# A transformer layer on eight cores: attention groups reordered, score banks rotated, a weight load and buffers re-placed

## The chip, the cores and the metric

The kernel runs on the 8 cores of one Trainium2 chip, each core with 2 of the 16 sequences and no traffic between cores. The metric is the device time of the slowest core in microseconds (us), lower is better.

## What is computed

One layer with the normalization behind each residual sum, for x of 16 x 2048 x 1024 (float32):

```python
q, k, v = x @ Wq, x @ Wk, x @ Wv                      # 1024 x 1024 each
scores = where(causal, q @ k.T, -inf) / 32            # 2048 x 2048 per sequence
x = layernorm(x + (softmax(scores) @ v) @ Wo)
h = silu(x @ (w_gate / 127).T) * (x @ (w_up / 127).T)  # hidden width 3072, int32 weights
x = layernorm(x + h @ (w_down / 127).T)
```

## The kernel before

P = 128, S = 2048, D = 1024; a sequence has 16 tiles t of 128 queries, in 4 groups g of four (NT = 16, NG = 4, ND = 8). All matmuls are bf16, 128 x 128 weights against up to 512 columns, into the banks of PSUM: banks 0 to 5 are `PF` (float32, `pf`), 6 and 7 are `PB` (bf16, `pbank`).

`emit_seq` (L333) runs twice, for sequence 0 and 1:

- POOL casts x to bf16 in DRAM and loads `wqb` and `wkb` (L340 to L344); SP loads x transposed, `xT`.
- Q and K projection (L356), each weight tile used for four matmuls in a row; then `wvb` is loaded on POOL (L372) into the place of wqb and wkb, so after the last K matmul; V projection (L380), two matmuls per weight tile.
- `wob`, the output projection's weights, is allocated and loaded on POOL right after V's part of the program (L391, L392), and in sequence 0 the three feed-forward weights are cast to bf16 in DRAM behind it (L395 to L397).
- Attention (L402 to L468). `emit_scores_softmax(t)`: g + 1 banks of scores, 8 matmuls each (L411), bank nb always in PSUM bank nb; the last, diagonal bank is scaled and masked by DVE (L416), the others copied by ACT (L421), all into `sc`; DVE takes the maximum (L425), ACT the exponential into `E` (L428), one of four slots j = t % 4. `emit_T(t)`: 4(g + 1) transposes of E on TensorE (L443), eight to a bank of PB, and a DVE copy into `ET` (L447). `emit_AV(g)`: 8 banks (4 and 5 in turn) of 4(g + 1) matmuls (L456), copied by DVE to `aoT` (L460).
- Output projection (L492) by tiles, with the residual sum (L497) and `emit_ln` (L316) on DVE and ACT; y goes to DRAM (SP, L501) and in bf16 (POOL, L503), and after tiles 7 and 15 SP loads half of it transposed, `yT` (L509).
- Gate and up (L543, L553) in 6 groups of weights `wgTb`, `wuTb` (SP transposes, L528, L532), product into `h`; down projection (L591) with `wdT` (SP transposes, L579), second `emit_ln`, output.

The order of attention is written out:

```python
for g in range(NG):
    for j in range(4):
        emit_scores_softmax(4 * g + j)
    for j in range(4):
        emit_T(4 * g + j)
    emit_AV(g)
```

What waits for what: each engine and each DMA queue works off its instructions in program order. `Builder.op` records for every operation what it must wait for by the keys it reads and writes; instructions on TensorE need not wait for one another. SBUF is laid out by `Arena`: `alloc` takes the start of the smallest free block that is large enough, `free` gives the range back and merges it with free neighbours, and the block then carries the pending operations of all that was in it. Whoever writes into a tensor allocated from the block waits for all of these (alias waits), even where the bytes themselves belonged to something else. 210,815 bytes a partition are handed out. Of them 17,056 hold constants and `xs`; then come xT (32,768), wqb and wkb (16,384 each), qT, kT and v (32,768 each), up to 180,896.

The functions that the change touches, and what calls them:

Of the kernel before, what the change touches and what calls it, by code (L numbers as in the profile page):

```python
# [205 lines left out]
class Arena:  # L206
# [9 lines left out]
        self.live = {}  # L216
        self.peak = 0

    def alloc(self, name, shape, dtype):
        nbytes = int(np.prod(shape[1:])) * mybir.dt.size(dtype)  # L220
        nbytes = (nbytes + 31) // 32 * 32
        for ent in sorted(self.free_list, key=lambda e: e[1]):
            if ent[1] >= nbytes:
                off = ent[0]
                deps = set(ent[2])
                ent[0] += nbytes
                ent[1] -= nbytes
                if ent[1] == 0:
                    self.free_list.remove(ent)
                for nm, (o2, n2) in self.live.items():  # L230
                    assert off + nbytes <= o2 or o2 + n2 <= off, \
                        f"arena overlap: {name}@({off},{nbytes}) vs {nm}@({o2},{n2})"
                h = self.nc.alloc_sbuf_tensor_at(name, list(shape), dtype, offset=self.base + off)
                self.live[name] = (off, nbytes)
                self.peak = max(self.peak, max(o + n for o, n in self.live.values()))
                self.b.add_alias_deps(name, deps)
                return h
        raise MemoryError(f"arena: no space for {name} ({nbytes}B/part); "
                          f"free={[(e[0], e[1]) for e in self.free_list]}")
# [17 lines left out]
def build_program():  # L257
# [6 lines left out]
    wo_d = nc.dram_tensor("wo", [D, D], F32, kind="ExternalInput")  # L264
# [24 lines left out]
    b = Builder(nc)  # L289
    ar = Arena(nc, b)  # L290
# [42 lines left out]
    def emit_seq(s):  # L333
# [41 lines left out]
        for t in range(NT):  # L375
# [7 lines left out]
            for half in range(2):  # L383
# [4 lines left out]
        ar.free("xT" + sfx)  # L388

        aoT = ar.alloc("aoT" + sfx, [P, ND, S], BF16)  # L390
        wob = ar.alloc("wob" + sfx, [P, ND, D], BF16)  # L391
        b.dma("pool", lambda e: e.dma_start(out=wob[:], in_=wo_d.ap().rearrange("(ec p) k -> p ec k", p=P)),  # L392
              writes=[("wob" + sfx,)], key="wo")
        if s == 0:
            b.dma("pool", lambda e: e.dma_start(out=wgbf_d.ap(), in_=wg_d.ap()), writes=[("wgbf",)], key="wgc")  # L395
            b.dma("pool", lambda e: e.dma_start(out=wubf_d.ap(), in_=wu_d.ap()), writes=[("wubf",)], key="wuc")
            b.dma("pool", lambda e: e.dma_start(out=wdbf_d.ap(), in_=wd_d.ap()), writes=[("wdbf",)], key="wdc")  # L397
        scb = ar.alloc("sc" + sfx, [P, S], F32)
        Eb = ar.alloc("E" + sfx, [P, 4, S], BF16)
        ET = ar.alloc("ET" + sfx, [P, NT, 512], BF16)  # L400

        def emit_scores_softmax(t):  # L402
            g = t // 4
            wlen = (g + 1) * 512
            j = t % 4
            sl = t % 2
            for nb in range(g + 1):
                ap, kk = pf(nb * 512, 512)
                for ec in range(ND):
                    b.op("pe", lambda e, ap=ap, ec=ec, t=t, nb=nb:  # L410
                         e.matmul(ap, qT[:, ec, t * P:(t + 1) * P], kT[:, ec, nb * 512:(nb + 1) * 512],  # L411
                                  start=(ec == 0), stop=(ec == ND - 1)),
                         reads=[("qT" + sfx, ec, t // 4), ("kT" + sfx, ec, nb)], writes=list(kk))
                if nb == g:
                    b.op("dve", lambda e, ap=ap, nb=nb, j=j:
                         e.scalar_tensor_tensor(scb[:, nb * 512:(nb + 1) * 512], ap, INV_SQRT_DK,  # L416
                                                maskt[:, j, :], ALU.mult, ALU.add),
                         reads=list(kk) + [("maskt", j)], writes=[("sc" + sfx, nb)])
                else:
                    b.op("act", lambda e, ap=ap, nb=nb:  # L420
                         e.activation(scb[:, nb * 512:(nb + 1) * 512], ap, AF.Copy, scale=INV_SQRT_DK),  # L421
                         reads=list(kk), writes=[("sc" + sfx, nb)])
            sckeys = [("sc" + sfx, nb) for nb in range(g + 1)]
            b.op("dve", lambda e, wlen=wlen, sl=sl:
                 e.reduce_max(nmax[:, sl:sl + 1], scb[:, 0:wlen], axis=AX.X, negate=True),  # L425
                 reads=sckeys, writes=[("nmax", sl)])
            b.op("act", lambda e, wlen=wlen, sl=sl, t=t, j=j:
                 e.activation(Eb[:, j, 0:wlen], scb[:, 0:wlen], AF.Exp, bias=nmax[:, sl:sl + 1], scale=1.0,  # L428
                              accum_out=rs_all[:, t:t + 1]),
                 reads=sckeys + [("nmax", sl)], writes=[("E" + sfx, j), ("rs", t)])  # L430

        def emit_T(t):
            g = t // 4
            ncs = 4 * (g + 1)
            j = t % 4
            for c0 in range(0, ncs, 8):
                cb = min(8, ncs - c0)
                half = (c0 // 8) % 2
                for ci in range(cb):
                    cs = c0 + ci  # L440
                    apb, kkb = pbank(half, ci * P, P)
                    b.op("pe", lambda e, apb=apb, cs=cs, j=j:
                         e.transpose(apb, Eb[:, j, cs * P:(cs + 1) * P], identb[:]),  # L443
                         reads=[("E" + sfx, j), ("identb",)], writes=list(kkb))
                apb, kkb = pbank(half, 0, cb * P)
                dst = ET[:, c0:c0 + cb, j * P:(j + 1) * P]
                b.op("dve", lambda e, dst=dst, apb=apb: e.tensor_copy(dst, apb),  # L447
                     reads=list(kkb), writes=[("ET" + sfx, c0 + ci, j) for ci in range(cb)])

        def emit_AV(g):  # L450
            ncs = 4 * (g + 1)
            for vc in range(ND):
                ap, kk = pf((4 + vc % 2) * 512, 512)
                for cs in range(ncs):
# [5 lines left out]
                b.op("dve", lambda e, ap=ap, vc=vc, g=g: e.tensor_copy(aoT[:, vc, g * 512:(g + 1) * 512], ap),  # L460
                     reads=list(kk), writes=[("aoT" + sfx, vc, g)])

        for g in range(NG):
            for j in range(4):
                emit_scores_softmax(4 * g + j)
            for j in range(4):
                emit_T(4 * g + j)
            emit_AV(g)  # L468
        b.op("dve", lambda e: e.reciprocal(ri_all[:], rs_all[:]),
             reads=[("rs", t) for t in range(NT)], writes=[("ri",)])  # L470

# [44 lines left out]
        ar.free("r1" + sfx)  # L516
        ar.free("y" + sfx)

        h_actT = ar.alloc("h" + sfx, [P, NH, S], BF16)
        wgTb = ar.alloc("wgTb" + sfx, [P, 2, ND, 512], BF16)  # L520
        wuTb = ar.alloc("wuTb" + sfx, [P, 2, ND, 512], BF16)
        sg = ar.alloc("sg" + sfx, [P, 2, 512], BF16)

        for hgrp in range(NH // 4):
            slw = hgrp % 2
# [118 lines left out]
```

How the kernel before makes its waits and increments, by code:

```python
            def body(eng):  # L167
                know = {}
                for o in ops_by_eng[eng_key]:
                    for d in sorted(o.deps):
                        p = ops[d]
                        if p.sem_id is None:
                            continue
                        v = eff_val(p, o.i)
                        if know.get(p.sem_id, 0) >= v:
                            continue
                        sem = dma_sems[p.sem_id[1]] if p.sem_id[0] == "d" else eng_sems[p.sem_id[1]]
                        eng.wait_ge(sem, v)
                        n_waits[0] += 1
                        know[p.sem_id] = v
                        for k, v2 in p.know.items():
                            if know.get(k, 0) < v2:
                                know[k] = v2
                    ins = o.fn(eng)
                    if o.sem_id is not None:
                        ins.then_inc(dma_sems[o.sem_id[1]] if o.sem_id[0] == "d" else eng_sems[o.sem_id[1]],
                                     16 if o.sem_id[0] == "d" else 1)
                    for k, v2 in o.know.items():
                        if know.get(k, 0) < v2:
                            know[k] = v2
                if eng_key == "sp":
                    for k in final_wait_keys:
                        if k in dma_counts and know.get(("d", k), 0) < dma_counts[k]:
                            eng.wait_ge(dma_sems[k], dma_counts[k])
```

## Time and profile before

| | us |
|---|---|
| median of 2 runs | 3381.49 (3380.61 to 3382.38) |
| the profiled execution | 3385.87 |
| its span on the slowest core (core 7) | 3384.3 |
| spans of the 8 cores | 3363.1 to 3384.3 |
| busy on core 7: TensorE, DVE, ACT | 2636.4, 510.9, 320.9 |
| mean granted TensorE clock | 0.746 |

The profile is that of core 7, unless a row says otherwise, with times from the start of its span. PE is TensorE (PEld its weight loads), DVE VectorE, ACT ScalarE, POOL GpSimd, SP SyncE; SPq is SP's queue. L411 is line 411 of the kernel. In a view of instructions, a line gives start, duration, engine, line, operation, output <- inputs and how many are merged into it; the bracket behind gives the engine's idle time just before and who ended it. In a view of windows, a line gives the stretch, its length, then busy time and number of instructions for PE, PEld, DVE, ACT and POOL, the clock granted to TensorE (1.00 is 2.4 GHz, 0.50 is 1.2 GHz), the DMA engines' busy share and GB/s. The trace misses a few matmul records, so "x5" behind "x3" may stand where there are more.

### The profile page before, as it was taken

How to read it: one execution, taken by the hardware profiler on the slowest of the kernel's cores; microseconds unless marked ns; L12 is line 12 of the kernel's file. 1: busy time of each engine (PE TensorE's matmuls, PEld its weight loads, DVE VectorE, ACT ScalarE, POOL GpSimd, SP SyncE). 2: the span in 40 equal slices, each digit the busy share in tenths (PEclk: the TensorE clock that was granted, in tenths of full speed). 3: DMA queues.
4: the chain of work that ended last, by engine and by line, in shares of the span. 5: the costliest groups of instructions: out<-in, count | busy, mean ns of one | idle time of the engine just before them, and what ended most of it. 6: DMA issues, size and time to landing. Idle time of an engine off the chain costs nothing.

```text
span 3384.3 us, 34352 instructions; the slowest of 8 cores (3363.1 to 3384.3 us)
## 1 busy us (share of the span) xinstructions
PE 2636.4 (78%) x8256; PEld 808.4 (24%) x8256; DVE 510.9 (15%) x754; ACT 320.9 (9%) x629; POOL 32.0 (1%) x60
## 2 busy tenths in 40 slices
PE   0779777878870999977966787778788739999599
PEld 0323111111110333322322331111111113333144
DVE  0000211110330111111220001110103211111033
ACT  0212000010000111100001220000100001111000
POOL 0000000000000000000000000000000000000000
PEclk9988555555555999988988995555555559999799
DMA  9129900000457211123243110000004551110423
GB/s 121 35 38 118 112 6 0 0 0 0 118 124 121 45 35 26 26 42 90 88 99 63 21 30 0 0 0 0 0 0 109 118 110 31 26 37 15 81 89 104
DMA packets 254654, 176.31 MB, mean 52 GB/s; under 512 B 224976, under 2 KB 224976, under 8 KB 253648
## 3 DMA queue, kind: packets, MB, share of 16 engines
q1 hardware_dynamic: 240640, 121.68, 15.3%
q0 software_dynamic: 13840, 52.43, 11.6%
q8 instruction: 94, 1.54, 0.2%
q14 instruction: 80, 0.66, 0.1%
HBM read 121.63 MB, written 69.21 MB: 56 GB/s over the span
## 4 chain that ended last, share of the span: by engine, by line
PE 75%; issue 8%; SPq 7%; DMA 6%; DVE 2%; ACT 1%; POOL 0%; DVEq 0%; ACTq 0%; POOLq 0%
PE PF L543 12%; PE PF L553 12%; PE PF L456 11%; PE PF L591 11%; PE PF L411 11%; PE PF L356 7%; PE PF L492 6%; PE PF L380 4%; SPq L347 3%; PE PB L443 2%; SPq L509 2%; SPq L579 2%; DMA xs<-x 2%; DMA xbf<-x 1%; DMA wgTb_s<-wgbf 1%
## 5 line engine op out<-in xcount | busy, mean ns | idle before, releaser
L543 PE MATMUL PF<-yT_s,wgTb_s 128*128 128x512 bf16 x1536 | 413.6, 380 | 140.0 <-DMA wgTb_s<-wgbf 140.0
L456 PE MATMUL PF<-ET_s,v_s 128*128 128x512 bf16 x640 | 365.0, 588 | 89.2 <-DVE ET_s L447 3.2
L591 PE MATMUL PF<-wdT_s,h_s 128*128 128x512 bf16 x1536 | 370.6, 381 | 81.8 <-DMA wdT_s<-wdbf 81.8
L411 PE MATMUL PF<-kT_s,qT_s 128*128 128x512 bf16 x640 | 359.3, 582 | 89.3 <-DVE sc_s L416 5.7
L553 PE MATMUL PF<-yT_s,wuTb_s 128*128 128x512 bf16 x1536 | 410.3, 376 | 0.0
L492 PE MATMUL PF<-wob_s,aoT_s 128*128 128x512 bf16 x512 | 290.0, 590 | 78.5 <-DVE r_s L497 11.6
L356 PE MATMUL PF<-xT_s,wqb_s 128*128 128x512 bf16 x512 | 123.9, 388 | 165.1 <-DMA xT_s<-xbf 156.6
L565 DVE TENSOR_TENSOR h_s<-PF,sg_s 128x512 bf16<-128x512 f32 x192 | 123.7, 686 | 788.9 <-PE PF L553 781.5
L543 PEld LDWEIGHTS PF<-yT_s,wgTb_s 128*128 128x128 bf16 x1536 | 146.7, 96 | 392.7 <-issue 303.8
L591 PEld LDWEIGHTS PF<-wdT_s,h_s 128*128 128x128 bf16 x1536 | 149.1, 97 | 303.1 <-issue 168.8
L553 PEld LDWEIGHTS PF<-yT_s,wuTb_s 128*128 128x128 bf16 x1536 | 146.7, 96 | 249.2 <-issue 159.2
L416 DVE SCALAR_TENSOR_TENSOR sc_s<-PF,maskt 128x512 f32<-128x512 f32 x32 | 22.1, 692 | 972.7 <-PE PF L411 877.6
L562 ACT ACTIVATE sg_s<-PF 128x512 bf16<-128x512 f32 x192 | 104.2, 594 | 670.1 <-PE PF L543 670.0
L380 PE MATMUL PF<-wvb_s,xT_s 128*128 128x512 bf16 x512 | 134.9, 384 | 37.0 <-DMA wvb_s<-wv 37.0
L456 PEld LDWEIGHTS PF<-ET_s,v_s 128*128 128x128 bf16 x640 | 66.6, 105 | 384.5 <-issue 383.4
L411 PEld LDWEIGHTS PF<-kT_s,qT_s 128*128 128x128 bf16 x640 | 66.1, 105 | 381.0 <-issue 379.4
L356 PE MATMUL PF<-xT_s,wkb_s 128*128 128x512 bf16 x512 | 120.8, 379 | 8.2 <-ACT kT_s L361 2.4
L492 PEld LDWEIGHTS PF<-wob_s,aoT_s 128*128 128x128 bf16 x512 | 51.3, 105 | 316.8 <-issue 316.3
L443 PE MATMUL PB<-identb,E_s 128*128 128x128 bf16 x320 | 81.4, 266 | 50.4 <-DVE ET_s L447 9.8
L356 PEld LDWEIGHTS PF<-xT_s,wqb_s 128*128 128x128 bf16 x512 | 50.7, 99 | 237.6 <-issue 189.2
L460 DVE CAST aoT_s<-PF 128x512 bf16<-128x512 f32 x64 | 44.3, 692 | 410.5 <-PE PF L456 410.5
L325 ACT ACTIVATE lnl<-mv,epsb 128x1 f32<-128x1 f32 x64 | 18.8, 294 | 915.7 <-DVE mv L321 915.7
(42 smaller groups left out, 687.1 us busy)
## 6 DMA issues: line engine op xcount, KB each, us to landing
xs<-x SPq DMA_DIRECT2D x32, 512.0 KB, 5.2
ydram<-y_s SPq DMA_DIRECT2D x32, 512.0 KB, 3.0
ys_s<-ydram SPq DMA_DIRECT2D x32, 512.0 KB, 4.1
out<-outb_s SPq DMA_DIRECT2D x32, 512.0 KB, 2.9
xbf<-x POOLq DMA_DIRECT2D x2, 4096.0 KB, 41.2
ybf<-y_s POOLq DMA_DIRECT2D x32, 256.0 KB, 6.3
wgbf<-wg POOLq DMA_DIRECT2D x1, 6144.0 KB, 86.8
wubf<-wu POOLq DMA_DIRECT2D x1, 6144.0 KB, 142.4
```

Source lines behind the costliest of these rows:

```text
L347: b.dma("sp", lambda e, dc=dc: e.dma_start_transpose(xT[:, dc, :], xbf_dram.ap()[:, dc * P:(dc + 1) * P]), reads=[("xbf",)], writes=[("xT" ...
L356: e.matmul(ap, wb[:, ec, m * P:(m + 1) * P], xT[:, ec, n * 512:(n + 1) * 512], start=(ec == 0), stop=(ec == ND - 1)),
L380: e.matmul(ap, xT[:, ec, t * P:(t + 1) * P], wvb[:, ec, half * 512:(half + 1) * 512], start=(ec == 0), stop=(ec == ND - 1)),
L411: e.matmul(ap, qT[:, ec, t * P:(t + 1) * P], kT[:, ec, nb * 512:(nb + 1) * 512], start=(ec == 0), stop=(ec == ND - 1)),
L443: e.transpose(apb, Eb[:, j, cs * P:(cs + 1) * P], identb[:]),
L456: e.matmul(ap, vtm[:, cs, vc * P:(vc + 1) * P], ET[:, cs, :], start=(cs == 0), stop=(cs == ncs - 1)),
L492: e.matmul(ap, aoT[:, vc, t * P:(t + 1) * P], wob[:, vc, half * 512:(half + 1) * 512], start=(vc == 0), stop=(vc == ND - 1)),
L543: e.matmul(apg, wgTb[:, slw, dc, hl * P:(hl + 1) * P], yT[:, dc, n * 512:(n + 1) * 512], start=(dc == 0), stop=(dc == ND - 1)),
L553: e.matmul(apu, wuTb[:, slw, dc, hl * P:(hl + 1) * P], yT[:, dc, n * 512:(n + 1) * 512], start=(dc == 0), stop=(dc == ND - 1)),
L562: b.op("act", lambda e, apg=apg, n=n: e.activation(sg[:, n % 2, :], apg, AF.Silu, scale=DEQ), reads=list(kkg), writes=[("sg" + sfx, n % 2)])
L565: e.tensor_tensor(h_actT[:, hc, n * 512:(n + 1) * 512], apu, sg[:, n % 2, :], ALU.mult),
L591: e.matmul(ap, h_actT[:, hc, t * P:(t + 1) * P], wdT[:, hc, half * 512:(half + 1) * 512], start=(hc == 0), stop=(hc == NH - 1)),
```

## The change

1. Attention: `emit_T` and `emit_AV` of group g are put behind the first `emit_scores_softmax` of group g + 1 (those of the last group come at the end). E gets a fifth slot and is used by t % 5.
2. `score_bank`: group 0 uses PSUM bank t % 2, group 1 banks 0, 1 and 2, 3 in turn, groups 2 and 3 as before.
3. `wob` is allocated, and its load issued on POOL, after attention's tensors are freed.
4. `Arena.alloc` can take the end of the highest free block (`side="top"`); yT, wgTb, wuTb and sg use it.
5. `PHASE_STOP`, an empty string, guards two early returns that aren't taken.

The diff, without the bodies of the two early returns:

```diff
--- before.py
+++ after.py
@@ -27,6 +27,8 @@
 INV_SQRT_DK = 1.0 / 32.0
 DEQ = 1.0 / 127.0
 EPS = 1e-5
+
+PHASE_STOP = ""
 
 BLOCK_METHOD = {"pe": "tensor", "act": "scalar", "dve": "vector", "pool": "gpsimd", "sp": "sync"}
 
@@ -216,15 +218,22 @@
         self.live = {}
         self.peak = 0
 
-    def alloc(self, name, shape, dtype):
+    def alloc(self, name, shape, dtype, side="bottom"):
         nbytes = int(np.prod(shape[1:])) * mybir.dt.size(dtype)
         nbytes = (nbytes + 31) // 32 * 32
-        for ent in sorted(self.free_list, key=lambda e: e[1]):
+        cands = sorted(self.free_list, key=(lambda e: -e[0]) if side == "top" else (lambda e: e[1]))
+        for ent in cands:
             if ent[1] >= nbytes:
-                off = ent[0]
+                if side == "top":
+                    off = (ent[0] + ent[1] - nbytes) // 32 * 32
+                    if off < ent[0]:
+                        continue
+                    ent[1] = off - ent[0]
+                else:
+                    off = ent[0]
+                    ent[0] += nbytes
+                    ent[1] -= nbytes
                 deps = set(ent[2])
-                ent[0] += nbytes
-                ent[1] -= nbytes
                 if ent[1] == 0:
                     self.free_list.remove(ent)
                 for nm, (o2, n2) in self.live.items():
@@ -388,16 +397,21 @@
         ar.free("xT" + sfx)
 
         aoT = ar.alloc("aoT" + sfx, [P, ND, S], BF16)
-        wob = ar.alloc("wob" + sfx, [P, ND, D], BF16)
-        b.dma("pool", lambda e: e.dma_start(out=wob[:], in_=wo_d.ap().rearrange("(ec p) k -> p ec k", p=P)),
-              writes=[("wob" + sfx,)], key="wo")
         if s == 0:
             b.dma("pool", lambda e: e.dma_start(out=wgbf_d.ap(), in_=wg_d.ap()), writes=[("wgbf",)], key="wgc")
             b.dma("pool", lambda e: e.dma_start(out=wubf_d.ap(), in_=wu_d.ap()), writes=[("wubf",)], key="wuc")
             b.dma("pool", lambda e: e.dma_start(out=wdbf_d.ap(), in_=wd_d.ap()), writes=[("wdbf",)], key="wdc")
         scb = ar.alloc("sc" + sfx, [P, S], F32)
-        Eb = ar.alloc("E" + sfx, [P, 4, S], BF16)
+        Eb = ar.alloc("E" + sfx, [P, 5, S], BF16)
         ET = ar.alloc("ET" + sfx, [P, NT, 512], BF16)
+
+        def score_bank(t, nb):
+            g = t // 4
+            if g == 0:
+                return t % 2
+            if g == 1:
+                return 2 * (t % 2) + nb
+            return nb
 
         def emit_scores_softmax(t):
             g = t // 4
@@ -405,7 +419,7 @@
             j = t % 4
             sl = t % 2
             for nb in range(g + 1):
-                ap, kk = pf(nb * 512, 512)
+                ap, kk = pf(score_bank(t, nb) * 512, 512)
                 for ec in range(ND):
                     b.op("pe", lambda e, ap=ap, ec=ec, t=t, nb=nb:
                          e.matmul(ap, qT[:, ec, t * P:(t + 1) * P], kT[:, ec, nb * 512:(nb + 1) * 512],
@@ -424,10 +438,10 @@
             b.op("dve", lambda e, wlen=wlen, sl=sl:
                  e.reduce_max(nmax[:, sl:sl + 1], scb[:, 0:wlen], axis=AX.X, negate=True),
                  reads=sckeys, writes=[("nmax", sl)])
-            b.op("act", lambda e, wlen=wlen, sl=sl, t=t, j=j:
-                 e.activation(Eb[:, j, 0:wlen], scb[:, 0:wlen], AF.Exp, bias=nmax[:, sl:sl + 1], scale=1.0,
+            b.op("act", lambda e, wlen=wlen, sl=sl, t=t:
+                 e.activation(Eb[:, t % 5, 0:wlen], scb[:, 0:wlen], AF.Exp, bias=nmax[:, sl:sl + 1], scale=1.0,
                               accum_out=rs_all[:, t:t + 1]),
-                 reads=sckeys + [("nmax", sl)], writes=[("E" + sfx, j), ("rs", t)])
+                 reads=sckeys + [("nmax", sl)], writes=[("E" + sfx, t % 5), ("rs", t)])
 
         def emit_T(t):
             g = t // 4
@@ -439,9 +453,9 @@
                 for ci in range(cb):
                     cs = c0 + ci
                     apb, kkb = pbank(half, ci * P, P)
-                    b.op("pe", lambda e, apb=apb, cs=cs, j=j:
-                         e.transpose(apb, Eb[:, j, cs * P:(cs + 1) * P], identb[:]),
-                         reads=[("E" + sfx, j), ("identb",)], writes=list(kkb))
+                    b.op("pe", lambda e, apb=apb, cs=cs, t=t:
+                         e.transpose(apb, Eb[:, t % 5, cs * P:(cs + 1) * P], identb[:]),
+                         reads=[("E" + sfx, t % 5), ("identb",)], writes=list(kkb))
                 apb, kkb = pbank(half, 0, cb * P)
                 dst = ET[:, c0:c0 + cb, j * P:(j + 1) * P]
                 b.op("dve", lambda e, dst=dst, apb=apb: e.tensor_copy(dst, apb),
@@ -460,12 +474,22 @@
                 b.op("dve", lambda e, ap=ap, vc=vc, g=g: e.tensor_copy(aoT[:, vc, g * 512:(g + 1) * 512], ap),
                      reads=list(kk), writes=[("aoT" + sfx, vc, g)])
 
+        pend = [None]
         for g in range(NG):
             for j in range(4):
                 emit_scores_softmax(4 * g + j)
-            for j in range(4):
-                emit_T(4 * g + j)
-            emit_AV(g)
+                if j == 0 and pend[0] is not None:
+                    pg = pend[0]
+                    pend[0] = None
+                    pg()
+            def mk(g=g):
+                def run():
+                    for j in range(4):
+                        emit_T(4 * g + j)
+                    emit_AV(g)
+                return run
+            pend[0] = mk()
+        pend[0]()
         b.op("dve", lambda e: e.reciprocal(ri_all[:], rs_all[:]),
              reads=[("rs", t) for t in range(NT)], writes=[("ri",)])
 
@@ -476,9 +500,21 @@
         ar.free("E" + sfx)
         ar.free("ET" + sfx)
 
...
+        wob = ar.alloc("wob" + sfx, [P, ND, D], BF16)
+        b.dma("pool", lambda e: e.dma_start(out=wob[:], in_=wo_d.ap().rearrange("(ec p) k -> p ec k", p=P)),
+              writes=[("wob" + sfx,)], key="wo")
         r1 = ar.alloc("r1" + sfx, [P, 2, D], F32)
         ybuf = ar.alloc("y" + sfx, [P, 4, D], F32)
-        yT = ar.alloc("yT" + sfx, [P, ND, S], BF16)
+        yT = ar.alloc("yT" + sfx, [P, ND, S], BF16, side="top")
 
         for t in range(NT):
             sl = t % 2
@@ -516,10 +552,15 @@
         ar.free("r1" + sfx)
         ar.free("y" + sfx)
 
...
         h_actT = ar.alloc("h" + sfx, [P, NH, S], BF16)
-        wgTb = ar.alloc("wgTb" + sfx, [P, 2, ND, 512], BF16)
-        wuTb = ar.alloc("wuTb" + sfx, [P, 2, ND, 512], BF16)
-        sg = ar.alloc("sg" + sfx, [P, 2, 512], BF16)
+        wgTb = ar.alloc("wgTb" + sfx, [P, 2, ND, 512], BF16, side="top")
+        wuTb = ar.alloc("wuTb" + sfx, [P, 2, ND, 512], BF16, side="top")
+        sg = ar.alloc("sg" + sfx, [P, 2, 512], BF16, side="top")
 
         for hgrp in range(NH // 4):
             slw = hgrp % 2
```

## Rows read from the trace of the kernel before

**Rows 1.** The page: busy time by engine, and the chain that ended last.
```profile
PE 2636.4 (78%) x8256; PEld 808.4 (24%) x8256; DVE 510.9 (15%) x754; ACT 320.9 (9%) x629; POOL 32.0 (1%) x60
...
PE 75%; issue 8%; SPq 7%; DMA 6%; DVE 2%; ACT 1%; POOL 0%; DVEq 0%; ACTq 0%; POOLq 0%
```

**Rows 2.** Windows: attention, the stretch before gate/up, gate/up, before the down projection.
```profile
316.30:832.20 515.90, 401.43 (x801) 82.55 (x801) 70.58 (x87) 38.80 (x58) 0.00 (x0) 0.50 0.21 25
...
1035.00:1101.00 66.00, 0.00 (x0) 0.00 (x0) 0.00 (x0) 0.00 (x0) 0.00 (x0) 0.50 0.79 117
1101.00:1500.00 399.00, 397.73 (x1536) 146.69 (x1536) 61.37 (x96) 53.39 (x97) 0.00 (x0) 0.99 0.13 28
1500.00:1542.00 42.00, 0.76 (x2) 0.27 (x3) 0.49 (x1) 0.00 (x0) 0.00 (x0) 0.53 0.92 162
```

**Rows 3.** Waits, whole span: engine, line, waited for, us in total, times, longest.
```profile
PE PB L443 <- DVE ET_s L447: 9.8, 12, 0.9
PE PF L411 <- DVE sc_s L416: 5.7, 6, 1.0
```

**Rows 4.** Instructions in order of time, TensorE, scores of group 0, sequence 0.
```profile
316.34 4.05 PE L411 MATMUL PF<-kT_s,qT_s 128*128 128x512 bf16 x8
...
328.00 2.79 PE L411 MATMUL PF<-kT_s,qT_s 128*128 128x512 bf16 x4 [0.94 <-DVE sc_s L416]
...
334.67 3.52 PE L411 MATMUL PF<-kT_s,qT_s 128*128 128x512 bf16 x5 [0.94 <-DVE sc_s L416]
```

**Rows 5.** Windows: scores and T of group 0, scores of t=4, AV of group 3.
```profile
316.30:340.20 23.90, 16.88 (x34) 3.22 (x33) 4.13 (x6) 3.62 (x8) 0.00 (x0) 0.60 1.08 121
340.20:349.00 8.80, 4.26 (x17) 1.60 (x16) 2.98 (x6) 0.81 (x2) 0.00 (x0) 0.50 0.77 86
...
370.00:381.10 11.10, 9.01 (x18) 1.61 (x16) 0.69 (x1) 0.60 (x1) 0.00 (x0) 0.50 0.86 97
...
740.90:832.20 91.30, 73.38 (x129) 13.42 (x129) 5.53 (x8) 0.00 (x0) 0.00 (x0) 0.50 0.00 0
```

**Rows 6.** Windows of core 4 (sequence 1), then core 6 (sequence 0): first score tiles.
```profile
2001.90:2006.00 4.10, 3.03 (x9) 0.68 (x7) 0.00 (x0) 1.16 (x2) 0.00 (x0) 1.00 0.00 0
2006.00:2009.20 3.20, 1.68 (x5) 0.48 (x5) 1.38 (x2) 0.82 (x2) 0.00 (x0) 0.99 0.00 0
2009.20:2012.60 3.40, 2.08 (x4) 0.31 (x3) 0.69 (x1) 0.00 (x0) 0.00 (x0) 0.50 0.00 0
...
316.80:317.75 0.95, 0.00 (x1) 0.03 (x1) 0.73 (x2) 0.00 (x0) 0.00 (x0) 1.00 0.88 103
317.75:320.60 2.85, 2.10 (x6) 0.54 (x6) 0.64 (x1) 0.82 (x2) 0.00 (x0) 0.99 0.19 23
```

**Rows 7.** Instructions in order of time: end of the scores of t=15, first transposes.
```profile
716.59 1.55 PE L443 MATMUL PB<-identb,E_s 128*128 128x128 bf16 x4
...
717.69 2.29 DVE L425 TENSOR_REDUCE nmax<-sc_s 128x1 f32<-128x2048 f32 x1
```

**Rows 8.** The same for TensorE, sequence 1: first score matmul, first transpose.
```profile
2016.99 4.05 PE L411 MATMUL PF<-kT_s,qT_s 128*128 128x512 bf16 x8
...
2039.79 0.72 PE L443 MATMUL PB<-identb,E_s 128*128 128x128 bf16 x2
```

**Rows 9.** The same, sequence 0: last AV matmul, first of the output projection.
```profile
831.87 0.58 PE L456 MATMUL PF<-ET_s,v_s 128*128 128x512 bf16 x1
832.25 2.83 PE L492 MATMUL PF<-wob_s,aoT_s 128*128 128x512 bf16 x4
```

**Rows 10.** The same, both sequences: first matmul of V's projection.
```profile
248.77 1.44 PE L380 MATMUL PF<-wvb_s,xT_s 128*128 128x512 bf16 x3 [19.01 <-DMA wvb_s<-wv]
...
1949.97 2.29 PE L380 MATMUL PF<-wvb_s,xT_s 128*128 128x512 bf16 x5 [17.98 <-DMA wvb_s<-wv]
```

**Rows 11.** DMA issues (count, KB, median us to landing), and the spread for wqb.
```profile
wvb_s<-wv POOLq DMA_DIRECT2D x2, 2048.0 KB, 17.8
wob_s<-wo POOLq DMA_DIRECT2D x2, 2048.0 KB, 28.2
...
DMA to landing us min/median/max: 20.1/38.3/56.6
```

**Rows 12.** Instructions in order of time, SP's queue: transposes into yT, second half.
```profile
1034.07 44.59 SPq L509 DMA_TRANSPOSE yT_s<-ybf  x8
```

More of the change, by code:

```diff
@@ L477, in emit_seq @@
         ar.free("ET" + sfx)
+        if PHASE_STOP == "B":
+            for vc in range(ND):
+                b.dma("pool", lambda e, vc=vc: e.dma_start(out=out_d.ap()[s, vc * P:(vc + 1) * P, 0:1024],
+                                                         in_=aoT[:, vc, 0:1024]),
+                      reads=[("aoT" + sfx, vc, g) for g in range(NG)], key=f"ost{s % 2}")
+            for nm in ("aoT", "wob"):
+                ar.free(nm + sfx)
+            return
+        wob = ar.alloc("wob" + sfx, [P, ND, D], BF16)
+        b.dma("pool", lambda e: e.dma_start(out=wob[:], in_=wo_d.ap().rearrange("(ec p) k -> p ec k", p=P)),
+              writes=[("wob" + sfx,)], key="wo")
         r1 = ar.alloc("r1" + sfx, [P, 2, D], F32)
         ybuf = ar.alloc("y" + sfx, [P, 4, D], F32)
-        yT = ar.alloc("yT" + sfx, [P, ND, S], BF16)
+        yT = ar.alloc("yT" + sfx, [P, ND, S], BF16, side="top")
         for t in range(NT):
@@ L517, in emit_seq @@
         ar.free("y" + sfx)
+        if PHASE_STOP == "C":
+            for nm in ("r1", "y", "yT"):
+                ar.free(nm + sfx)
+            return
         h_actT = ar.alloc("h" + sfx, [P, NH, S], BF16)
-        wgTb = ar.alloc("wgTb" + sfx, [P, 2, ND, 512], BF16)
-        wuTb = ar.alloc("wuTb" + sfx, [P, 2, ND, 512], BF16)
-        sg = ar.alloc("sg" + sfx, [P, 2, 512], BF16)
+        wgTb = ar.alloc("wgTb" + sfx, [P, 2, ND, 512], BF16, side="top")
+        wuTb = ar.alloc("wuTb" + sfx, [P, 2, ND, 512], BF16, side="top")
+        sg = ar.alloc("sg" + sfx, [P, 2, 512], BF16, side="top")
         for hgrp in range(NH // 4):
```

## The prediction

> **What bounds the kernel now.** I read the busy line and the chain first: TensorE is busy for 78% of the span, and the chain that ended last is 75% TensorE [rows 1]. So every microsecond in which TensorE waits or runs slowly counts in full, while DVE (15%) and ACT (9%) only matter where TensorE waits for them. Then I read the stages by windows [rows 2]. Gate/up runs at a granted clock of 0.99, the 2.4 GHz level; its 1536 matmuls in 399 us take 0.26 us each. Attention (scores, transposes, AV) runs at 0.50, the 1.2 GHz level, for 515.9 us, and again in the second sequence. The rest that stands out is idle time behind DMA, as the 66 us ahead of gate/up and the 42 us ahead of the down projection. The change touches attention and the place of one load, so those two carry the sum.
>
> **Attention in detail.** Is TensorE waiting there? Nearly not: in both sequences together it waits 5.7 us (6 times) for a score bank and 9.8 us (12) for the copy of transposed tiles [rows 3]; a wait for an exponential isn't listed at all. What makes attention long is the clock. Here every matmul has its own weights. Eight of them take 4.20 us at the upper level (4.05 from 316.34 and the usual 0.15 to the next: 0.525 each) [rows 4], and 5.55 us at the lower (two banks of t=4 in 11.1 us: 0.695 each) [rows 5]. The first tile of a sequence runs at the upper level. Then comes a hole of 0.95 us until DVE has emptied the only score bank, and soon after the clock is down.
>
> When exactly does it fall? On core 4, in the second sequence, the window of the first tile (2001.9 to 2006.0) still shows 1.00, the hole follows, and the fall comes only at 2009.2. On core 6 it is 0.99 until 320.6, after a hole at 316.8 [rows 6]. I went through both sequences on all eight cores, 16 cases: in none does the clock fall before the first hole. But no hole-free run of these matmuls at the upper level is longer than one tile, so nothing here shows whether a longer one keeps it.
>
> **The parts.**
>
> (a) *Order: T and AV of group g-1 stand behind the first score tile of group g.* This can cover a wait for the softmax, and there is none to cover: after t=15, where the chain is longest (DVE's maximum alone takes 2.29 us), TensorE goes into the transposes of t=12 at 716.59 with no idle time [rows 7], and has three tiles of them to do before it needs the last exponential. Gain 0. Cost: the ET copies now queue on DVE behind the mask and the maximum of t=4g. For group 0 only four transposes run first (1.6 us); the mask takes 0.69 and the maximum over 1024 at most the 2.29 of 2048, so at most 1.3 us are waited where 0.7 are now. For the other groups 8 or 16 transposes run first. I take 0 and keep 1 us for the range. The fifth E buffer makes the order legal and costs no time.
>
> (b) *Score banks t%2 in group 0.* Three holes per sequence go. A cold tile with its hole takes 6.67 us from start to start (328.00 to 334.67) [rows 4], 5.55 without: 1.1 each, the warm one 0.95, so 3.1 per sequence and **6.3 us** in both (a little more than the waits' 5.7, since weight loads start late too). Banks 2 and 3 in group 1 remove nothing: its tiles follow each other without a wait now.
>
> (c) *The clock, which follows from (b) and (a).* The scores of t=0 to 3 and, by the new order, the two banks of t=4 now run without a hole: six banks, 48 matmuls. If the level holds as it does within a tile, they take 6 x 4.20 = 25.2 us. Today: 23.9 + 11.1 = 35.0 in the first sequence [rows 5], and 22.8 (2016.99 to 2039.79) + 11.1 = 33.9 in the second [rows 8]. Gain 9.8 + 8.7 = **18.5 us**, (b) included. Then come 16 transposes with copies between them (4.26 us of TensorE in 8.8 us), a thinner load than what loses the clock today, so I let it fall there. It doesn't come back: AV of group 3, 128 matmuls in 91.3 us, stays at 0.50 throughout [rows 5].
>
> The Trainium skill (TensorE: Matmul & The Clock Gate, Part 4) says that transposes don't count as activity for the clock. By that rule it falls at the first block of T as well; in this trace transposes stand only at 0.50, which neither proves nor denies it.
>
> (d) *wob's load moves behind attention.* This is the cost. The arena has 210,815 bytes a partition. Now wob lies at 180,896, right behind v, in bytes that nobody used before, and is loaded 600 us before its reader. After the change sc (8,192) and E (20,480) take the place behind v, up to 209,568, and wob is allocated once qT, kT, v, sc, E and ET are freed. These merge into one free block that carries the pending operations of all; its first bytes, at 49,824, were ET's. So the DMA waits on POOL for the last AV matmul, and the first matmul of the output projection waits for the DMA. Today that matmul follows AV without idle time [rows 9]. What it will be like, V's projection shows: wvb has the same size, queue and cast and is awaited in the same way, and TensorE sits idle for 19.01 and 17.98 us [rows 10]. Sum **+37.0 us**, all of it on the path: behind wob, POOL has only the ybf stores, which wait for TensorE's results anyway, and SP and DVE have nothing to do until the first tile is multiplied. Bounds: today wob is queued right behind wvb, 0.9 us later, and lands 28.2 + 0.9 - 17.8 = 11.3 us after it, which leaves out the start of a load: 22.6 for two. The quickest wqb lands after 20.1, with some 0.7 to the matmul 20.8: 41.6 for two [rows 11]. I take wvb's, the nearest in kind. The three weight casts on POOL go out 0.9 us earlier; their readers start 800 us later.
>
> (e) *Places of yT, wgTb, wuTb and sg.* wgTb's transposes stand on SP behind the eight of yT, which take 44.6 us from 1034.07 [rows 12] and fill most of the idle stretch; by then the output projection is done, so no other place brings them earlier. h now lies over aoT, wob and y, whose readers are done before gate/up starts. wdT, and xT and wqb of the second sequence, still meet a merged block that holds the last gate/up or down matmul. The idle stretches stay: 0. PHASE_STOP is empty: 0.
>
> **Sum.** +37.0 - 18.5 = +18.5 us. Against the profiled execution, 3385.9 us (span 3384.3 and 1.6 around it), that is 3404.4. That execution lies 4.4 us above the median of the runs, 3381.5, so for the median I predict **3400.0 us**.
>
> **Rivals.**
>
> *B, the clock falls as now.* A longer run may lose it by itself, hole or not, since one such matmul takes 0.525 us where gate/up's take 0.26, so the array has half the work. Against it: no fall before a hole in 16 cases. Then only (b) is won: 3381.5 + 37.0 - 6.3 = 3412.2.
>
> *C, faster.* With fewer holes the clock stays up in all of attention. 1280 score and AV matmuls would take 0.525 instead of some 0.705 (0.695 for scores, 91.3 / 128 = 0.713 for AV): -230, and 3381.5 + 37.0 - 230 = 3188.5. It decides as soon as the blocks of T don't lower the clock. Against it: they are thinner than anything that runs at the upper level, and the steady AV of group 3 doesn't win it back.
>
> The Trainium skill (TensorE: Matmul & The Clock Gate, Part 1) says that activity releases the throttle. By that rule steady AV would be at the upper level, and C would come out. The trace disagrees: 0.50 in 91.3 us.
>
> *D, slower by over 2%.* wob's load is slow where it now stands, as all eight cores ask for it at once. Price: the slowest wqb took 56.6 us [rows 11], so 2 x 56.6 - 6.3 = +107, 3488. It decides from about 37 us a load. Against it: the cores fetch wvb together too, and the DMA share in the stretch ahead is 0.00 [rows 5].
>
> *E, the load is hidden.* It would need a place that is free earlier; the merged block says no. Then 3381.5 - 18.5 = 3363.0.
>
> **Chances.** A, the forecast, 0.60; B 0.27; C 0.05; D 0.04; E 0.04. A reaches from 3385.6 (22.6 for the loads) to 3405.6 (41.6, and 1 us of (a)), B from 3397.8 to 3417.8. The range 3386 to 3418 holds both and leaves out the other three and a little more. 2% is 67.6 us, about what a measurement can tell from no change: A, B and E lie within it (0.91), C below (0.05), D above (0.04).
>
> **What would show it.** Two waits of the output projection for DMA wob, of 18 to 19 us; no wait of scores for DVE in group 0; the granted clock at 1.00 for some 25 us of attention instead of 5 to 8 (in B as now), then 0.50 to its end; T of group 0 with a wait of at most 1.3 us for its first copy; the idle stretches as now. I'd be wrong if wob isn't awaited, if AV runs at 1.00 anywhere, or if a new wait stands on TensorE within attention.

## The result and the profile after

The change makes the kernel slower: 3488.2 us (median of 11 runs; 3487.5 of the eight fast ones), 1.0317 times before (95% interval 1.0272 to 1.0363). The profiled execution took 3487.2 us with a span of 3485.3, 101.0 us more than before. The forecast was 3400.0, range 3386 to 3418. Every version also has slower executions, in which a die runs at a lower clock: ratios, later medians and the stage table leave them out (or that die's cores), and the table's last column takes only executions with all cores at the full clock.

What TensorE waits for (view of waits, after: engine, line, waited for, us in total, times, longest). L365 is the Q and K projection, L389 V, L528 the output projection, L584 gate, L632 the down projection.

```profile
PE PF L365 <- DMA xT_s<-xbf: 168.0, 2, 99.9
PE PF L584 <- DMA wgTb_s<-wgbf: 165.8, 2, 84.7
...
PE PF L632 <- DMA wdT_s<-wdbf: 126.1, 2, 83.8
...
PE PF L389 <- DMA wvb_s<-wv: 35.1, 2, 19.9
PE PF L528 <- DMA wob_s<-wo: 29.2, 2, 15.0
PE PF L528 <- DVE r_s L533: 25.0, 3, 20.1
PE PB L457 <- DVE ET_s L461: 11.3, 12, 1.4
```

The same view before has 156.6 for xT, 140.0 for wgTb, 81.8 for wdT and 11.6 for the output projection's wait on DVE:

```profile
PE PF L356 <- DMA xT_s<-xbf: 156.6, 2, 98.2
PE PF L543 <- DMA wgTb_s<-wgbf: 140.0, 2, 85.5
...
PE PF L591 <- DMA wdT_s<-wdbf: 81.8, 2, 42.0
...
PE PF L492 <- DVE r_s L497: 11.6, 3, 5.6
```

The four grew by 11.4, 25.8, 44.3 and 13.4 us: 94.9. Add 29.2 for wob and take off 1.9 for wvb, and 20.7 that attention gained (below): 101.5, the span's difference to half a microsecond. So the loss stands in waits for transposed data, in places that the change hardly seems to touch.

Attention itself, TensorE in order of time:

```profile
319.02 23.51 PE L425 MATMUL PF<-kT_s,qT_s 128*128 128x512 bf16 x48
342.37 1.31 PE L457 MATMUL PB<-identb,E_s 128*128 128x128 bf16 x4
345.13 1.09 PE L457 MATMUL PB<-identb,E_s 128*128 128x128 bf16 x3 [1.45 <-DVE ET_s L461]
...
838.07 0.58 PE L528 MATMUL PF<-wob_s,aoT_s 128*128 128x512 bf16 x1 [14.17 <-DMA wob_s<-wo]
...
2024.38 8.16 PE L425 MATMUL PF<-kT_s,qT_s 128*128 128x512 bf16 x17
...
2544.59 3.52 PE L528 MATMUL PF<-wob_s,aoT_s 128*128 128x512 bf16 x5 [14.99 <-DMA wob_s<-wo]
```

and the windows around its start:

```profile
319.00:344.00 25.00, 17.98 (x53) 4.81 (x51) 6.77 (x10) 5.03 (x11) 0.00 (x0) 1.00 0.96 105
344.00:355.00 11.00, 5.93 (x17) 1.71 (x17) 2.70 (x6) 1.24 (x2) 0.00 (x0) 0.50 1.25 141
```

48 score matmuls follow each other without a hole, in 23.4 us, at 1.00, and so they do on all eight cores and in both sequences. With the transposes the clock falls to 0.50 and stays there, where [rows 5] have 0.60 for the first 23.9 us. From the first score matmul to the last of AV it is 838.07 - 14.17 - 319.02 = 504.9 us, before 515.9; in the second sequence 505.2, before 514.9. That is the gain of 11.0 + 9.7 = 20.7.

Now SP's queue, in order of time: eight transposes into yT, a few of wgTb and wuTb, and the 24 of wdT, all of sequence 1.

```profile
2642.88 26.22 SPq L545 DMA_TRANSPOSE yT_s<-ybf  x8
...
2787.98 1.11 SPq L569 DMA_TRANSPOSE wgTb_s<-wgbf  x1
2790.61 1.11 SPq L573 DMA_TRANSPOSE wuTb_s<-wubf  x1
2793.24 1.11 SPq L569 DMA_TRANSPOSE wgTb_s<-wgbf  x1
...
3227.20 80.23 SPq L620 DMA_TRANSPOSE wdT_s<-wdbf  x24
```

Before, the same stretches of sequence 1 are

```profile
2630.45 11.07 SPq L509 DMA_TRANSPOSE yT_s<-ybf  x8
...
2745.54 1.11 SPq L528 DMA_TRANSPOSE wgTb_s<-wgbf  x1
2746.69 1.22 SPq L532 DMA_TRANSPOSE wuTb_s<-wubf  x1
2749.25 1.11 SPq L528 DMA_TRANSPOSE wgTb_s<-wgbf  x1
...
3168.29 37.18 SPq L579 DMA_TRANSPOSE wdT_s<-wdbf  x24
```

One transpose of yT takes 3.3 us instead of 1.4, one of wdT 3.3 instead of 1.5, and those of wgTb and wuTb follow each other every 2.7 us instead of every 1.6 (mean of the first 16 steps). And SP itself waits for them (waits of SP's queue, after):

```profile
SPq L180 <- DMA wgTb_s<-wgbf: 90.8, 74, 3.2
SPq L180 <- DMA wuTb_s<-wubf: 80.9, 65, 3.0
SPq L180 <- DMA wdT_s<-wdbf: 53.4, 24, 2.7
...
SPq L180 <- DMA yT_s<-ybf: 34.2, 15, 3.7
```

It also waits 27.9 us (7 times) for xT. Before, SP waited 21.7 us (44 times) for wgTb, 23.2 (42) for wuTb, 2.4 (once) for wdT and isn't listed for yT or xT. In sequence 0 after the change all keep their old pace (24 of wdT in 38.3 us, before in 38.5). That gives the theory:

**W, stale waits.** `Arena` never forgets pending operations of a block that is not used up to the last byte, and adds them up at each merge. Before, E and ET together fill exactly the free block behind aoT, whose list holds xT's transposes; a block that is used up goes, and its list with it. Also, wob stood between two blocks, whose lists stayed apart. After, ET takes half of that block, the other half keeps the list, and once attention is freed everything from there to the end of the arena is one block with all lists. So in sequence 1 yT, wgTb, wuTb, wdT and xT carry, among others, their own namesakes' transposes of sequence 0. Such a wait would be met long ago, but transposes have coarse keys, for which the value is counted anew at every operation:

```python
def eff_val(p, oi):
    if p.dma_key in self.coarse_keys:
        return 16 * bisect.bisect_left(key_idx[p.dma_key], oi)
    return p.val
```

It is the number of all DMAs with this key ahead of the waiting one, the DMA just issued among them. So each transpose waits until the one before it has landed. In the emitted program SP gets 7 such waits each for xT and both halves of yT, and 23 for wdT, all in sequence 1, where the kernel before has none. Those of wgTb wait for the last one of wgTb in both kernels, and those of wuTb likewise, so that one of each can be on its way. After the change each waits for the last one of the other tensor too (95 waits, all in sequence 1), and only one is on its way.

The emitted programs also tell which edits bring the waits. The kernel before with `side="top"` and nothing else gets wgTb's waits for wuTb and the 23 of wdT; with the late wob as well it gets all of them. The late wob alone can't be laid out, as no free block then holds the 98,304 bytes of h. The fifth slot of E plays no part.

**P, the rival.** The new places of yT, wgTb, wuTb and wdT in SBUF make transposes slow, with the waits as a mere sign of it.

The stages side by side, from the traces (start of a stage's first matmul to the end of its last, us, median of the eight cores, and in brackets the pause until the next stage; e5, e6, e7b and the second execution of before by cores 0 to 3). The last column is the span of the median core, and of several executions the median (for e2 and e7b there is only one). It is steadier than the slowest core, and small differences below are read from it.

```
        Q,K       V   attention     out      gate/up    down      Q,K       V   attention     out      gate/up    down   span
before  132(+17)  68  516( 0)   183(+83)   398(+40)  203(+58)  130(+16)  67  515( 0)   184(+55)   398(+38)  168   3370.4
 (e8)   133(+18)  68  516( 0)   183(+84)   398(+42)  203(+57)  130(+16)  67  515( 0)   183(+50)   397(+38)  168
after   132(+17)  68  505(+14)  183(+84)   396(+40)  202(+66)  131(+14)  68  505(+14)  198(+83)   398(+82)  168   3477.8
e1      132(+18)  68  505(+15)  183(+83)   397(+43)  202(+58)  131(+15)  67  505(+14)  184(+49)   397(+39)  168   3374.8
e2      132(+17)  68  516( 0)   183(+85)   397(+39)  202(+68)  131(+16)  68  516( 0)   198(+83)   397(+79)  168   3468.4
e3      131(+16)  68  505( 0)   183(+85)   397(+43)  202(+58)  130(+15)  68  505( 0)   183(+49)   397(+40)  168   3345.1
e4      132(+17)  68  508( 0)   183(+83)   398(+39)  202(+57)  130(+16)  67  508( 0)   184(+51)   397(+38)  168   3355.5
e5      131(+16)  68  517( 0)   183(+85)   396(+41)  203(+58)  130(+15)  67  517( 0)   184(+49)   397(+41)  168   3371.2
e6      131(+17)  68  392( 0)   184(+85)   397(+41)  202(+57)  130(+15)  68  392( 0)   183(+49)   397(+41)  169   3119.6
e7b     132(+16)  68  392( 0)   167(+92)   397(+43)  202(+57)  130(+15)  68  392( 0)   166(+58)   397(+40)  168   3101.0
e7      131(+15)  68  392( 0)   103(+83)   396(+41)  202(+57)  130(+15)  67  392( 0)   102(+51)   396(+40)  168   2960.7
```

### The profile page after: what moved, and what is told of

Read it like the earlier page. It is cut to its first block, busy times and chain, and to the rows that moved or that the text cites. A ratio compares the mean times of both kernels' runs of the same rounds, so it can differ in the third digit from the quotient of the medians.

```text
span 3485.3 us, 36431 instructions; the slowest of 8 cores (3463.7 to 3485.3 us)
## 1 busy us (share of the span) xinstructions
PE 2619.2 (75%) x8256; PEld 807.0 (23%) x8256; DVE 510.9 (15%) x754; ACT 320.9 (9%) x629; POOL 32.0 (1%) x60
## 4 chain that ended last, share of the span: by engine, by line
PE 72%; DMA 13%; issue 8%; SPq 4%; DVE 2%; ACT 1%; POOL 0%; DVEq 0%; ACTq 0%; POOLq 0%
PE PF L584 11%; PE PF L594 11%; PE PF L470 11%; PE PF L632 11%; PE PF L425 10%; PE PF L365 7%; PE PF L528 5%; PE PF L389 4%; DMA wdT_s<-wdbf 2%; PE PB L457 2%; DMA xT_s<-xbf 2%; DMA xs<-x 2%; DMA yT_s<-ybf 1%; SPq L545 1%; SPq L356 1%
## 5 line engine op out<-in xcount | busy, mean ns | idle before, releaser
L584 PE MATMUL PF<-yT_s,wgTb_s 128*128 128x512 bf16 x1536 | 413.3, 379 | 165.8 <-DMA wgTb_s<-wgbf 165.8
L632 PE MATMUL PF<-wdT_s,h_s 128*128 128x512 bf16 x1536 | 370.3, 381 | 126.1 <-DMA wdT_s<-wdbf 126.1
L425 PE MATMUL PF<-kT_s,qT_s 128*128 128x512 bf16 x640 | 342.8, 558 | 83.6
L528 PE MATMUL PF<-wob_s,aoT_s 128*128 128x512 bf16 x512 | 289.9, 589 | 121.1 <-DMA wob_s<-wo 29.2
L365 PE MATMUL PF<-xT_s,wqb_s 128*128 128x512 bf16 x512 | 124.3, 389 | 176.5 <-DMA xT_s<-xbf 168.0
L584 PEld LDWEIGHTS PF<-yT_s,wgTb_s 128*128 128x128 bf16 x1536 | 146.7, 96 | 417.8 <-issue 331.6
L632 PEld LDWEIGHTS PF<-wdT_s,h_s 128*128 128x128 bf16 x1536 | 148.9, 97 | 347.4 <-issue 212.4
L389 PE MATMUL PF<-wvb_s,xT_s 128*128 128x512 bf16 x512 | 135.6, 386 | 35.1 <-DMA wvb_s<-wv 35.1
L528 PEld LDWEIGHTS PF<-wob_s,aoT_s 128*128 128x128 bf16 x512 | 51.3, 105 | 359.7 <-issue 359.1
L365 PE MATMUL PF<-xT_s,wkb_s 128*128 128x512 bf16 x512 | 120.8, 379 | 8.5 <-ACT kT_s L370 2.7
L457 PE MATMUL PB<-identb,E_s 128*128 128x128 bf16 x320 | 80.7, 264 | 51.9 <-DVE ET_s L461 11.3
L365 PEld LDWEIGHTS PF<-xT_s,wqb_s 128*128 128x128 bf16 x512 | 50.7, 99 | 249.4 <-issue 201.3
L474 DVE CAST aoT_s<-PF 128x512 bf16<-128x512 f32 x64 | 44.3, 692 | 411.2 <-PE PF L470 400.7
```

The source lines that it names most:

```text
L365: e.matmul(ap, wb[:, ec, m * P:(m + 1) * P], xT[:, ec, n * 512:(n + 1) * 512], start=(ec == 0), stop=(ec == ND - 1)),
L389: e.matmul(ap, xT[:, ec, t * P:(t + 1) * P], wvb[:, ec, half * 512:(half + 1) * 512], start=(ec == 0), stop=(ec == ND - 1)),
L457: e.transpose(apb, Eb[:, t % 5, cs * P:(cs + 1) * P], identb[:]),
L528: e.matmul(ap, aoT[:, vc, t * P:(t + 1) * P], wob[:, vc, half * 512:(half + 1) * 512], start=(vc == 0), stop=(vc == ND - 1)),
L584: e.matmul(apg, wgTb[:, slw, dc, hl * P:(hl + 1) * P], yT[:, dc, n * 512:(n + 1) * 512], start=(dc == 0), stop=(dc == ND - 1)),
L632: e.matmul(ap, h_actT[:, hc, t * P:(t + 1) * P], wdT[:, hc, half * 512:(half + 1) * 512], start=(hc == 0), stop=(hc == NH - 1)),
```

## The experiments

**e1, the stale waits are taken out of the changed kernel.** In both places where waits are derived from dependencies (here the first):

```diff
+                if p.dma_key in self.coarse_keys and know.get(p.sem_id, 0) >= p.val:
+                    continue
                 v = eff_val(p, o.i)
```

> The changed kernel, but a wait for a DMA of a coarse key is left out where the engine has already waited for a count that covers that DMA (such as those of sequence 0, seen from sequence 1). Buffers, their places, the order and wob's late load stay. Theory W (stale alias waits put the transposes of sequence 1 one behind the other): the three stretches of sequence 1 shrink back, down projection 0 to Q projection 1 from 270.6 to 261 us, output projection to gate/up from 283.5 to 239, gate/up to down projection from 481.6 to 437, together -98 us: about 3390 us, eight yT transposes in 11 us. Rival P (the places of yT, wgTb, wuTb, wdT at the end of SBUF make transposes slow): unchanged, 3488 us, transposes of yT in 25 us.

Measured: 3382.0 us, 0.9998 times before (0.9979 to 1.0017): the loss is gone, with every buffer in its new place. The median core's span is 103.0 less than after the change. SP's 24 transposes of wdT in sequence 1 are back at the old pace, 22 of them in

```profile
3169.57 35.92 SPq L624 DMA_TRANSPOSE wdT_s<-wdbf  x22
```

and TensorE's waits are near those of before (wgTb's is 9 us shorter), plus wob's:

```profile
PE PF L588 <- DMA wgTb_s<-wgbf: 130.6, 2, 82.1
PE PF L636 <- DMA wdT_s<-wdbf: 84.3, 2, 42.3
...
PE PF L532 <- DMA wob_s<-wo: 30.7, 2, 16.5
PE PF L532 <- DVE r_s L537: 11.9, 2, 6.1
```

P falls: the places are the same and the pace isn't. In the emitted program SP's transposes have the same DMA waits as in the kernel before. Elsewhere the edit goes further: it also drops stale waits of sequence 1 that the kernel before has, of ACT and DVE for the newest gate and up weights, and of the first load behind wdT for wdT.

**e2, the stale waits alone are put into the kernel before.**

```diff
                 deps = set(ent[2])
+                if name in ("xT_s1", "yT_s1", "wgTb_s1", "wuTb_s1", "wdT_s1"):
+                    deps |= self.ever
...
         deps = self.b.pending_ops_of(name)
+        if name in ("xT_s0", "yT_s0", "wgTb_s0", "wuTb_s0", "wdT_s0"):
+            self.ever |= deps
```

> The kernel before, with nothing but the pending operations of xT, yT, wgTb, wuTb and wdT of sequence 0 added to the alias waits of the same five in sequence 1. Theory W: the whole loss appears without any of the edits, 3381.5 + 98 = about 3480 us; attention and output projection keep their times. Rival P: no buffer moved, so 3381 us.

Measured: 1.0321 times before (1.0267 to 1.0374), which can't be told from the whole change's 1.0317; the profiled execution has a span of 3475.2, 90.9 more than before. By the table's last column the changed kernel is 9.4 slower than e2, near wob's 29.2 less the 20.7 of attention. TensorE's waits (the first is xT's, then wgTb's, wdT's and the output projection's on DVE):

```profile
PE PF L361 <- DMA xT_s<-xbf: 169.2, 2, 99.4
PE PF L548 <- DMA wgTb_s<-wgbf: 169.0, 2, 84.7
PE PF L596 <- DMA wdT_s<-wdbf: 116.7, 2, 78.1
...
PE PF L497 <- DVE r_s L502: 25.6, 2, 21.3
```

They grew by 12.6, 29.0, 34.9 and 14.0: 90.5 of the 90.9. SP's 24 transposes of wdT take

```profile
3221.78 75.90 SPq L584 DMA_TRANSPOSE wdT_s<-wdbf  x24
```

So the waits are enough to make the loss, and by e1 needed for it. The fourth figure is against the expectation, by which the output projection keeps its time. It is a second step of the same cause: SP needs 27.5 us instead of 11 for yT's first half, and the x tile of the output projection's ninth tile stands behind it.

**e3, wob early again.** e1, with the allocations in the order E, sc, wob, ET, which lets all four fit; wob takes the place of wqb, and its load goes out after the last V matmul, ahead of attention. The order alone wouldn't do: without e1's edit all the stale waits but those of xT would stay.

> e1_skip_old with E, sc, wob, ET allocated in this order, so that wob fits in the place of wqb and wkb and is loaded behind V, ahead of attention. Prices the late load by itself: the changed kernel's two waits for it sum to 29 us, so e1 minus 29, about 3361 us, which is also before minus 20 for score banks and clock. If the load's wait is partly paid elsewhere (the x loads or casts hide in it), the difference is smaller than 29.

Measured: 3355.0 us, 0.9922 times before (0.9891 to 0.9952). That is 27.0 less than e1, and 29.7 in the median core's span, where the two waits for wob sum to 30.7: the late load costs what TensorE waits for it, nearly all of it. e3 is the change as it may have been meant, and faster than the kernel before.

**e4, only the score banks** (`score_bank` of the change in the kernel before).

> The kernel before with the score banks of the change and nothing else: T and AV of group 0 stay ahead of t=4, so the run of score matmuls without a hole is four banks long, 16.8 us. Theory H (holes lose the clock): it stays at 1.00 over all four, 23.9 and 22.8 us become 16.8 each, -13 us: 3368. Theory of a clock that such matmuls lose anyway: only the holes go, -6 us: 3375.

Measured: 3362.3 us, 0.9939 (0.9915 to 0.9963). The four banks run without a hole (TensorE, in order of time, one core):

```profile
318.70 0.38 PE L419 MATMUL PF<-kT_s,qT_s 128*128 128x512 bf16 x1
319.23 15.20 PE L419 MATMUL PF<-kT_s,qT_s 128*128 128x512 bf16 x31
334.27 1.31 PE L451 MATMUL PB<-identb,E_s 128*128 128x128 bf16 x4
```

15.6 us from 318.70 to 334.27, which only the upper clock gives; it is 15.6 on all eight cores and in both sequences. Attention is 15.9 us shorter in both sequences together (507.7 each, before 516.1 and 515.2), where 13 were expected, and the median core's span 14.9: the gain is in attention. The pause before gate/up of sequence 1 is 55 us in the first profile of the kernel before and 51 here, see e8.

**e5, only the order** (e3 with each score bank where it was).

> e3 with every score bank where it was before the change (bank nb), so of the change there remain the order of T and AV, the fifth slot of E and the buffers' places, without stale waits and with wob loaded early. My theory, that the order covers no wait: the holes of group 0 are back and the clock falls after the first tile, so the time is that of the kernel before, 3382 us, within 0.2%. Rival, that the order hides something of softmax: faster than before by what e3 has over e4, some 6 us.

Measured: 3379.3 us, 0.9998 (0.9969 to 1.0026). The order by itself gains nothing; attention is 517 us, some 2 longer in each sequence. Its worth appears only together with the banks: e3's attention is 505 and e4's 508, since t=4's two banks still run on the upper clock. Between e3 and e5 only the banks differ: the same 48 matmuls take 23.4 us without holes (all cores, both sequences) and 35.0 to 36.1 with them (cores 0 to 3, both sequences).

**e6, scores in pairs** (e3, for each two banks):

```diff
-                for ec in range(ND):
...
+                if nb % 2 == 0:
+                    nbs = [n for n in (nb, nb + 1) if n <= g]
+                    for ec in range(ND):
+                        for n in nbs:
```

> e3 with the score matmuls of groups 1 to 3 in pairs: the same weights (a tile of q) against banks nb and nb + 1 in turn, as gate/up does; group 2's third bank stays single. Theory: what holds this stage at 1.2 GHz is that every matmul has its own weights. Pairs at the upper level take 0.26 us each, so a score tile of group 3 takes 8.4 us instead of 22.2, and the clock shows 1.00 in such stretches and 0.50 in T and AV. Of the 288 matmuls in groups 1 to 3 of a sequence 256 are paired: 0.695 to 0.26, -111 us, the other 32 to 0.525, -5; in two sequences -232 us less what each new rise of the clock costs: about 3140 us. Rival (the clock is down because of the waits on PSUM, not because of the weights): the level stays 0.50, pairs take about 0.43 to 0.48 each, -110 to -135 us, about 3235 us.

Measured: 3129.4 us, 0.9252 times before (0.9216 to 0.9287). Windows of core 1, sequence 0: scores of t=5 to 8, T and AV of group 1, scores of t=9 to 12, T and AV of group 2, scores of t=13 to 15, T and AV of group 3:

```profile
370.00:387.00 17.00, 15.96 (x61) 5.52 (x60) 5.74 (x6) 6.61 (x11) 0.00 (x0) 1.00 1.13 125
388.80:447.60 58.80, 43.23 (x92) 9.56 (x92) 8.53 (x12) 1.67 (x2) 0.00 (x0) 0.50 1.03 116
451.00:481.00 30.00, 26.87 (x97) 8.95 (x95) 7.33 (x6) 9.45 (x15) 0.00 (x0) 1.00 1.03 114
485.00:566.00 81.00, 63.38 (x132) 13.74 (x133) 8.55 (x14) 1.40 (x2) 0.00 (x0) 0.50 0.13 15
570.00:592.30 22.30, 22.30 (x88) 8.18 (x87) 5.96 (x4) 8.70 (x13) 0.00 (x0) 1.00 0.00 1
598.00:707.30 109.30, 85.26 (x176) 18.32 (x176) 9.46 (x14) 0.00 (x0) 0.00 (x0) 0.50 0.00 0
```

The clock goes up with each stretch of pairs and down with each of T and AV, whose code is untouched. So two matmuls to a weight tile bring the clock up in scores where one left it down. It isn't a wait on PSUM that went: of the scores only those of group 0 had one [rows 3], and it is those of groups 1 to 3 that are paired. Not separated is that pairs also write two banks in turn.

**e7b and e7, the output projection in pairs too,** without and with the x tile t + 1 issued on SP ahead of the stores of tile t.

```diff
-            for half in range(2):
-                for vc in range(ND):
+            for vc in range(ND):
+                for half in range(2):
```

> e6 with the output projection in pairs too (vc outside, the two halves inside). TensorE's 256 matmuls per sequence would take 67 us instead of 190. But SP issues the load of the next x tile only behind the store of y, and load, residual sum and normalization take 10.4 us per tile in the kernel before, against 11.1 us of matmuls: so the stage stays at some 170 us per sequence, and the gain over e6 is at most 20 us in all. If instead the loads do not bound it, the gain is 200 us and more.

> e7b with the x tile t + 1 issued ahead of the stores of tile t. Then a tile is bounded by DVE (3.9 us busy per tile, with its waits for ACT some 5) and TensorE (4.2 us): about 6 us per tile, 96 us per sequence instead of 200: some 200 us less than e6, about 2940 us.

Measured: e7b 0.926 (0.918 to 0.934), no difference from e6 that the ratios can tell. In its profile the stage shrinks from 184 to 167 us only, and the pause behind it grows by 7 and 9; the median core's span is 18.6 us below e6's, within the forecast's 20. e7 2971.1 us, 0.8783 times before (0.8754 to 0.8813), the stage 102 us. That is 158 less than e6 where 200 were forecast: the stage took 184 us in e6, not 200, and a tile takes 6.4 now, not 6. Waits of DVE show what bound e7b, the x tile:

```profile
DVE r_s L541 <- DMA xs<-x: 203.9, 30, 20.5
```

and e7 has 55.6 us (13 times) there. e7 is the fastest version measured.

**e8, the kernel before once more.**

> The kernel before once more, unchanged, for the spread of single stretches. In its first profile the pause before gate/up of sequence 1 was 56 us in the median of the cores; e3, e4 and e5, which touch nothing there, show 50. If 56 is a matter of the execution, this one shows some 50 and 3376 to 3382 us; if it belongs to the kernel, 56 again.

On cores 0 to 3 the pause is 50 us, the rest within 2 us of the first profile (attention 516, wdT's pauses 42 and 38). So 5 of the 55 us are a matter of the execution. Something smaller stays open. In the median core's span e4 gains what attention gains, but e1, e3 and e5 are some 4 us below what attention and wob explain (e3 25.3 less than before, 21.5 of it in attention). These three have both the new places and e1's edit. The table shows gate/up 1 us shorter and the pause before V 1 us shorter in e3; why, no run shows.

## Why the prediction was wrong, step by step

- **(a)** Right. The order covers nothing (e5). Its price, a wait of at most 1.3 us for group 0's first ET copy, is 1.45 us, a little over the bound.
- **(b), (c)** Right in mechanism and nearly in size: no hole before the transposes, the clock up to them and down for the rest. Forecast 18.5 us, measured 20.7; the matmuls took 0.487 us each (23.35 / 48) where the first tile had shown 0.525. Rival B and rival C are out; C's condition, AV at the upper level, doesn't occur in any of these runs.
- **(d)** Right place, too dear: 29.2 us for 37.0. I took wvb with wob queued behind it. With nothing behind, wob came in 14.2 and 15.0 us, between the lower bound of 11.3 and that row. wvb itself bears that out: in sequence 1 after the change nothing is queued behind it, and its wait is 15.2 us instead of 18.0; in sequence 0, where the weight casts follow it, it is still 19.9. The forecast without (e) would have been 3381.5 + 29.2 - 20.7 = 3390; e1, which is nearly that kernel, measured 3382.0.
- **(e)** Failed, and it is the whole miss. I wrote that the new places bring no new wait: "wdT, and xT and wqb of the second sequence, still meet a merged block that holds the last gate/up or down matmul". That is true of the latest operation in the list, and the latest is what usually counts. I didn't ask what else had come into the list, nor how the wait for it is counted. A dependency on a transpose of sequence 0 looks met since long; under `eff_val` it is a wait for the last DMA issued. Of the signs that I named, "the idle stretches as now" is the one that didn't hold. Cost 94.9 us in the two profiles (xT 11.4, output projection 13.4, wgTb 25.8, wdT 44.3), and 103.0 from e1 to the changed kernel in the median core's span; the profile of before had 5 us of pause too much, and e1 has the open 4.
- **Rivals and range.** The time agrees with rival D's 3488 by chance: its cause, a slow load of wob, isn't there. The range held only rivals that I had priced, and gave all waits outside attention but wob's a width of nothing, though the change re-placed fifteen buffers per sequence.

## What to carry to other kernels

When a change moves buffers, compare the waits that are emitted for each DMA before and after, in each pass of the outer loop, and not only the last operation that each place waits for: a wait that is met can still order a queue, where its value is counted at the place of the waiting instruction. Where a stage runs at the lower clock without waiting, look at how many matmuls share a weight tile before removing waits: here pairs were worth 226 us (e3 to e6), all holes and their effect on the clock 21. And when a stage's engine gets faster, look at what the queues do per tile (e7b) before counting the gain.

## What the runs showed of the hardware

- The clock outlasts 48 single-weight matmuls in a row at 0.487 us each (23.4 us, mean clock 1.00 in 16 cases of 16, after the change). With a hole of 0.95 us behind each of the first tiles it is lost on the way (mean clock before 0.60 to 0.67 over the first 32, 16 cases of 16; e5 0.56 to 0.61 over the 48, cores 0 to 3) [rows 6]. Once down it isn't raised by the same kind of matmul, even 128 in a row [rows 5]. Stretches of pairs raise it every time (e6).
- DMA transposes that wait for each other take 3.3 us each (1024 x 128, yT and wdT of sequence 1 after the change), those let go together 1.4 (yT) and 1.5 (wdT) before. From issue to landing it is 3.4 us then (median of those of wdT), so each is paid in full; before it is 4.6, and yet one goes out every 1.5.
- A 2 MB load with cast on POOL took TensorE 14.2 to 15.0 us of waiting with nothing queued behind it (wob, after; wvb 15.2), and 18.0 to 19.0 for wvb with wob behind it [rows 10].
